# Both norms of an expert stage computed by ScalarE with scales from GpSimd, and early loads on two queues

## The reference

```
h = tok(x)                              # 8 steps of relu(a + shift(state) @ W2.T + b2), both directions
h = h + attention(layernorm(h))         # 8 heads, scores exp(-gamma * |q-k|^2)
n = layernorm(h)
gate = top-2 softmax of n @ gate_w + gate_b
moe  = sum over 16 experts of gate * (relu(n @ w1 + b1) @ w2 + b2)
y = n + moe
h = h + layernorm(y) * gamma + beta
```

## Time and profile before

| | us |
|---|---|
| median of 3 runs | 873.78 |
| lowest and highest | 871.83, 874.65 |
| the profiled execution | 871.59 |
| its span in the trace | 869.0 |

### The profile page before, as it was taken

How to read it: one execution, slowest core, us unless ns; L and a number is a source line. 1 busy time by engine, 2 the same in 40 slices (tenths; PEclk the granted TensorE clock), 3 DMA queues, 4 the chain that set the end, 5 groups by cost and what they waited for, 6 DMA issues and landing times.

```text
span 869.0 us, 16981 instructions
## 1 busy us (share of the span) xinstructions
PE 766.4 (88%) x5712; PEld 438.4 (50%) x5712; DVE 702.2 (81%) x1810; ACT 491.1 (57%) x913; POOL 519.9 (60%) x719
## 2 busy tenths in 40 slices
PE   1699979999999999999999999899889899998894
PEld 1234346666666666666666665344344344444341
DVE  5376768999999999999999998577787877777652
ACT  0365668877887887888788785232333333333221
POOL 7260255445445344454454452469999999999867
PEclk9999979999999999999999999899999999999997
DMA  4300021111221112211112210000000000000000
GB/s 113 136 16 2 1 49 38 36 38 38 49 50 27 39 35 50 50 41 33 38 38 50 49 33 18 1 2 7 8 7 8 7 7 14 7 8 7 8 7 18
DMA packets 22789, 25.71 MB, mean 30 GB/s; under 512 B 12816, under 2 KB 21648, under 8 KB 22576
## 3 DMA queue, kind: packets, MB, share of 16 engines
q1 hardware_dynamic: 22384, 23.85, 11.5%
q10 hardware_dynamic: 320, 0.79, 0.4%
...
## 4 chain that ended last, share of the span: by engine, by line
PE 43%; DVE 33%; POOL 11%; issue 5%; ACT 3%; DMA 2%; SPq 1%; another core or an unknown queue 1%; POOLq 0%; DVEq 0%; ACTq 0%
DVE prob L753 15%; DVE m L769 9%; PE bank L1034 6%; PE bank L962 6%; PE bank L1149 6%; PE bank L1169 6%; PE bank L1082 5%; POOL cxn L425 5%; PE bank L1058 3%; PE bank L1060 2%; DVE qk L763 2%; POOL gated L436 2%; DVE wtok L877 2%; POOL cinv L421 2%; PE bank L1160 2%
## 5 line engine op out<-in xcount | busy, mean ns | idle before, releaser
L753 DVE TENSOR_SCALAR prob<-prob,cap_hi,cap_lo 125x250 f32<-125x250 f32 x512 | 232.7, 502 | 18.6 <-ACT prob L531 15.8
L401 POOL TENSOR_TENSOR sq<-sq 125x256 f32<-125x256 f32 x128 | 96.3, 759 | 170.7 <-ACT sq L545 126.7
L884 DVE SCALAR_TENSOR_TENSOR gated<-bank,nb,wb 128x500 f32<-128x500 f32 x160 | 115.7, 732 | 71.7 <-PE bank L1149 66.4
L1169 PE MATMUL bank<-gated,w_sb 64*64 64x500 f32 x1024 | 172.8, 594 | 0.0
L1149 PE MATMUL bank<-cs,w_sb 64*64 64x500 f32 x1024 | 170.4, 587 | 0.4 <-DVE gated L884 0.4
L531 ACT ACTIVATE prob<-bank 125x500 f32<-125x500 f32 x256 | 148.6, 591 | 38.0 <-PE bank L1060 35.0
L602 ACT ACTIVATE relu<-bank,b_sb 128x500 f32<-128x500 f32 x96 | 65.0, 678 | 175.1 <-PE bank L1149 170.5
L436 POOL TENSOR_TENSOR gated<-relu,wb 128x500 f32<-128x500 f32 x96 | 125.0, 1307 | 48.0 <-ACT relu L602 48.0
L1034 PE MATMUL bank<-prob,u 125*64 125x250 f32 x1024 | 125.8, 382 | 1.5
L1058 PE MATMUL bank<-m,s 128*125 128x500 f32 x256 | 111.0, 434 | 6.1 <-issue 6.1
L1060 PE MATMUL bank<-m,s 112*125 112x500 f32 x256 | 101.0, 395 | 0.0
...
## 6 DMA issues: line engine op xcount, KB each, us to landing
m<-m SPq DMA_DIRECT2D x128, 125.0 KB, 2.3
...
```

Source lines behind the costliest of these rows:

```text
L753: last = dve.tensor_scalar(part, part, cap_hi[0:T, h:h + 1], cap_lo[0:T, h:h + 1], ALU.min, ALU.max)
L884: dve.scalar_tensor_tensor(gated[g % 8][:, :], up_bank(g)[:, 0:C], nb1[:, g:g + 1], wb[q % 2][:, :], ALU.max, ALU.mult).then_inc(c_gated, 1)
L1169: last = pe.matmul(y[cols, 0:C], w2_sb[rows, g, :], gated[g % 8][rows, :], start=g == 1 and rows is HI, stop=v == 7, skip_group_check=True)
```

## The change

Four things are edited.

1. **Norms in stage C.** GpSimd no longer writes `cxn` and `yz`. A new `c_scales(q)`, behind group 1, takes the statistics of pair q and of pair q-4 together (one buffer `cagg` of 8 numbers a partition instead of twice 4) and makes -mean, var + eps, its power and their product. ScalarE then computes `scale * v + bias` with both as per-partition operands: `normed(p+1)`, four instructions on 125x128, and `result(p-3)`, four on 125x64, both in slot 1.
2. **Start, queues.** A_LOADS go from SyncE's queue to ScalarE's, ahead of W_LOADS; a one-element `Relu` stands between them, so that the function table is loaded there. SyncE's queue holds only `x_in`, `xparts`, the replicated copies and B_LOADS, and its wait for GpSimd's fills stands behind the write of `xparts`.
3. **Start, the copies.** The repeat is the second dimension of the source, not the first; rows of weights and constants are reordered to match.
4. **Start, fills.** GpSimd fills all four tails; VectorE's two fills are gone.

```diff
@@ constants
-            rows = slice(half + part * PARTS * D_IN, half + (part + 1) * PARTS * D_IN)
+            rows = slice(half + part, half + XROWS, PARTS)
@@ sync
             sp.dma_start(x_in[:, :, :], xin[:, :, :]).then_inc(a_xin, 16)
-            for dst, src in A_LOADS:
-                sp.dma_start(full(dst), full(src)).then_inc(ld_a, 16)
-
             sp.wait_ge(a_split, SPLIT)
-            sp.wait_ge(s_prepg, PREP_GX)
             sp.dma_start(xparts.rearrange("r p (q l) -> q r p l", q=128), x_part[:, :, :, :]).then_inc(a_scr, 16)
             sp.wait_ge(a_scr, 16)
+            sp.wait_ge(s_prepg, PREP_GX)
...
-                             src.unsqueeze(0).to_broadcast([PARTS, PARTS * D_IN, n * C])).then_inc(s, 16)
+                             src.unsqueeze(1).to_broadcast([PARTS * D_IN, PARTS, n * C])).then_inc(s, 16)
@@ gpsimd
-            done(gp.memset(xa[32:64, :].bitcast(F32), ONES2))
-            done(gp.memset(xw[32:64, :].bitcast(F32), ONES2))
+            for rows in (slice(32, 64), slice(96, 128)):
+                done(gp.memset(xa[rows, :].bitcast(F32), ONES2))
+                done(gp.memset(xw[rows, :].bitcast(F32), ONES2))
...
-            def c_normed(q):
...
+            def c_scales(q):
+
+                if valid(q):
+                    gp.wait_ge(c_ln, 2 * q + 2)
+                if valid(q - 4):
+                    gp.wait_ge(c_fin, 2 * (q - 4) + 2)
+                wait(gp, c_hn, min(q, PAIRS))
+                wait(gp, c_yz, q - 4)
+                gp.tensor_scalar(cneg[:, :, :], cagg[:, :, :, 0], -1.0, None, ALU.mult)
+                gp.tensor_tensor(cvar[:, :, :], cagg[:, :, :, 1], eps2[:, :, :], ALU.add).then_inc(c_inv, 1)
+                gp.wait_ge(c_inv, 3 * q + 1)
+                gp.tensor_tensor(cinv[:, :, :], cvar[:, :, :], mhalf2[:, :, :], ALU.pow).then_inc(c_inv, 1)
+                gp.wait_ge(c_inv, 3 * q + 2)
+                gp.tensor_tensor(cnb[:, :, :], cneg[:, :, :], cinv[:, :, :], ALU.mult).then_inc(c_inv, 1)
...
-                    if n == 0 and valid(p + 1):
-                        c_normed(p + 1)
+                    if n == 0:
+                        c_scales(p + 1)
@@ scalar
+            for dst, src in A_LOADS:
+                act.dma_start(full(dst), full(src)).then_inc(ld_a, 16)
+            act.wait_ge(a_table, 1)
+            act.activation(spare2[:, :], spare[:, :], ACT.Relu)
             act.wait_ge(a_xin, 16)
...
                 if v == 0:
+                    normed(0)
                     tokens_c(0)
...
+            def normed(q):
+
+                act.wait_ge(c_inv, 3 * q + 3)
+                wait(act, c_xt, q)
+                for c in range(CH):
+                    last = act.activation(cxn[:, c, :, :], h_all[:, q * CH + c, :].unsqueeze(1).to_broadcast([T, 2, D]),
+                                          ACT.Identity, bias=cnb[:, 0, c:c + 1], scale=cinv[:, 0, c:c + 1])
+                last.then_inc(c_hn, 1)
+
+            def result(q):
+
+                act.wait_ge(c_inv, 3 * (q + 4) + 3)
+                wait(act, c_gres, 2 * q - 1)
+                for c in range(CH):
+                    last = act.activation(yz[:, 0, c, :], yt[:, c, :], ACT.Identity, bias=cnb[:, 1, c:c + 1],
+                                          scale=cinv[:, 1, c:c + 1])
+                last.then_inc(c_yz, 1)
...
+                if v == 1 and valid(p + 1):
+                    normed(p + 1)
+                if v == 1 and valid(p - 3):
+                    result(p - 3)
@@ vector
-            dve.memset(xa[96:128, :].bitcast(F32), ONES2)
-            dve.memset(xw[96:128, :].bitcast(F32), ONES2)
+            dve.memset(spare[:, :], 0.0).then_inc(a_table, 1)
...
-                wait(dve, c_hn, q)
+                wait(dve, c_inv, 3 * q)
```

More of the change, by code:

```diff
@@ L127, in build @@
         wtok = sb("wtok", [T, CH, E, R])
-        cvar, cinv, cxn = sb("cvar", [T, CH]), sb("cinv", [T, CH]), sb("cxn", [T, CH, 2, D])
+        cagg, cvar = sb("cagg", [T, 2, CH, 2]), sb("cvar", [T, 2, CH])
+        cneg, cinv, cnb, cxn = sb("cneg", [T, 2, CH]), sb("cinv", [T, 2, CH]), sb("cnb", [T, 2, CH]), sb("cxn", [T, CH, 2, D])
+        eps2, mhalf2 = sb("eps2", [T, 2, CH]), sb("mhalf2", [T, 2, CH])
         cs1 = [sb(f"cs1_{j}", [128, C]) for j in range(3)]
@@ L620, in _ @@
             slot_c(0, 7)
-            for p in range(1, PAIRS + 2):
+            for p in range(1, PAIRS + 3):
                 for v in range(8):
```

55 lines of the change are left out of this document (19 added, 36 removed).

## The result

| | us |
|---|---|
| before, median of 4 runs beside it (range) | 872.81 (869.67 to 874.65) |
| after, median of 4 runs (range) | 950.52 (947.66 to 955.08) |
| ratio, 95% interval | 1.0899 (1.0841 to 1.0957) |
| span of the profiled execution, before and after | 869.0 and 950.0 |

The change made the kernel 78 us slower. The forecast was 918 with a range of 887 to 939: the direction held and so did half of the mechanism, the size did not. So the profile after is read for where the other 32 us are.

What follows compares the result with a forecast made beforehand. TensorE was taken to bound stage C, with GpSimd nearly full. Terms -9 + 48 + 1.5 - 0.5 + 4 + 1.5 = +45.5 us gave 917 on the profiled 871.6, 919 on the median 873.8; 918 taken, range 887 to 939.

Steps and rivals of the forecast that it cites:

- piece B: Stage C period after the extra matmuls (L1160): +0.85 us of collision each period, plus 1.2 for the lower clock.
- the collision: After the extra matmuls: freed GpSimd's product of group 9 delays VectorE's step until wtok, +0.85 us a period (0 if missed).
- the clock: Stage C: TensorE's longer idle time brings the lower clock in some eight periods of ten, +1.2 us a period (0 to 2.5).
- start, at step 1 of stage A: Copies spread and issued sooner, weights landing at 18.0, clock gain up to 2: -9 us (bounds -4.5 and -10.5).
- end of stage B: First two token norms on ScalarE, normed(0) and normed(1), delay the end of stage B: together +4 us (1 to 6).
- period 1, period 2: Stage C: period 1 has no y_low yet and gains 0.5 us on cxn; period 2 has only normed, +1.5.
- periods 3 to 14: Stage C periods with both norms: 12 x (1.95 + 0.85 + 1.2) = 12 x 4.0 = +48 us.
- period 15: Stage C before the change, without GpSimd's cxn: read as a trial, 22.23 us against 19.12; no term in the sum.
- from the relu of group 1 of period 16 to the end: Very end of the kernel: ScalarE's last result stands ahead of the last y_low, +1.5 us (-1 to +3).
- Piece A: Stage C, relu of group 1 to the extra matmuls (L1160): y_low queues behind ScalarE's norms, 9.0 to 9.1 against 7.15, +1.95 us.
- The faster rival: Stage C: ScalarE's queue never reaches y_low, TensorE's 1.17 us is gained in 13 periods: 850 us, chance 0.11.
- cheap ScalarE instructions: Stage C rival: eight norm instructions take 1.2 us, piece A falls to +0.76: 904, or 890 without clock loss; chance 0.13.

Runs made afterwards that it cites:

- queue_only: Kernel before with only A_LOADS on ScalarE's queue, the table load and the fills changed, copies in their old form: 872.1 us, ratio 0.9995.
- start_only: Kernel before with only the change's start (queues, table load, fills, copies), expert stage as before: 865.9 us, ratio 0.9937.
- early4: early2 with the token norm of pairs 0 and 1 on GpSimd as before: 841.1 us, ratio 0.9634 to the kernel before.
- early2: Kernel before plus new start, token norm on ScalarE with scales a period early, y_moe before group 5, GpSimd's yz before product 9, results after 12: 844.5 us, 0.9690.
- tail_late: Changed kernel with GpSimd's last two result steps moved from behind the product of group 9 to behind that of group 12: 916.5 us, 1.0508 to before.
- gp_spacer: Changed kernel plus three useless tensor_scalar instructions on GpSimd ahead of its product of group 9: 895.9 us, ratio 1.0290 to the kernel before.
- spacer_tt: Changed kernel plus three useless tensor_tensor instructions on GpSimd ahead of its product of group 9: 978.9 us, ratio 1.1206 to the kernel before.
- fill_short: Changed kernel plus four useless matmuls at each of TensorE's two waits (extra matmuls, wtok transposes): 926.4 us, ratio 1.0618 to the kernel before.

## Why the prediction was wrong

The steps that failed are the two terms of piece B: the collision, put at +0.85 us a period, is +1.84 with the clock up, and the clock, put at +1.2, is 2.5, since a second wait, for `wtok`, was not in the sum. Step by step, on the spans (869.0 and 950.0; +81.0 in all, where the sum had +45.5):

| step | forecast | measured |
|---|---|---|
| start, at step 1 of stage A | -9 | -9.7 |
| end of stage B | +4 | +4.4 |
| period 1, period 2 | -0.5, +1.5 | -1.8, +2.4 |
| periods 3 to 14 | +48 | +76.6 |
| period 15 | none | +4.3 |
| from the relu of group 1 of period 16 to the end | +1.5 | +4.9 |

- *Start*: right in size, in part by luck. The copies landed soon, as said. The DMA share was 0.85 from 16 to 18 us and 1.04 from 18 to 20 where near 0.7 was expected; other transfers ran beside the copies, so no run shows the share of the copies alone. The weights landed 3 us earlier than taken (15.15 for 18.0), and TensorE waited last for the copies, 0.34 us, not for the weights. The "up to 2" of clock was not there: the first `xa` matmuls behind 21.06 take 0.59 to 0.62 us, as before, though the clock column shows 1.00, and 0.37 from 25.10 on. One error made up for the other. Moving the loads gave nothing in the time by itself (`queue_only`), though 3.1 us at step 1.
- *End of stage B*: about right. The 4.4 is the difference between -9.7 and the -5.3 us at which the expert stage's first relu of group 1 stands, and 1.3 of it `start_only` loses too, without the norms. `early4` against `early2` puts the first two norms alone at 2.3 us by that relu (537.55 against 539.83) and at 3 to 5 by times and ratios.
- *Piece A*: right, 9.2 for 9.05 to 9.1. Power 1.66 (1.5 taken, in the bounds), `cxn` to the relu of group 4 2.88 (2.75), `y_low` at 7.86 (7.8). The faster rival needed 5.4 there and is out; so is the one of cheap ScalarE instructions, whose 1.2 us for eight no row had shown. TensorE's wait for `cxn` stayed at 0.71, where under 0.5 was expected.
- *Piece B, collision, +0.85: the first step that failed.* It was read from L866 of period 15 alone, and fits that period by luck. There L866, L870 and L873 are held, 0.98 + 0.27 + 0.53 = 1.78 us, where the usual period of before has 0.95 (L873 0.53, `wtok` 0.42); the difference is the 0.82 by which `wtok`'s transposes are late. `wtok` itself was free in period 15, since it began just ahead of a product:

```profile
831.53 0.68 DVE L877 TENSOR_TENSOR wtok<-lg 125x512 f32<-125x512 f32 x1
831.61 1.72 POOL L436 TENSOR_TENSOR gated<-relu,wb 128x500 f32<-128x500 f32 x1 [0.73 <-ACT relu L602]
```

  So it is in the six periods of after where the slower clock put the product of group 12 off (4.93 us, third row of the pieces). In the other six `wtok` is held too: 0.98 + 0.27 + 0.53 + 1.01 = 2.79 us, 1.84 more than before, as the third row shows (5.95 against 4.11). The collision and the clock were added as if they did not touch. That period 15 also had a wait of 1.48 us for `wtok` where 0.83 is usual was passed over. `tail_late`, `gp_spacer` and `spacer_tt` show the holds.
- *Piece B, clock, +1.2: the second.* For the wait that was foreseen it is about right: a fall behind `y_moe`'s wait came in 8 of 12 periods, and in six of them costs 24.52 - 23.01 = 1.5 us, since the late product then spares `wtok` (4.93 in place of 5.95). Not foreseen was a second fall, behind `wtok`'s wait of 2.67: in 6 of 12 periods, at 26.04 - 23.01 = 3.0. Together 2.5 a period, as `fill_short` shows. Without the extra holds there is no such wait and no such fall: `gp_spacer`, whose filler keeps them away, won 55 us.
- Together: (1.84 - 0.85) + (2.5 - 1.2) = 2.3 us, and 2.4 with piece A's 0.1, in 12 periods the 28.6 of the 35.5 missing. *Period 15* (+4.3) and the *end* (+3.4 over the forecast) make up the rest: the sum had set period 15 to nothing, as if the trial were itself unchanged, while ScalarE's `yz` and the wait of 2.67 with its lower clock come there too.
- *Range*: the clock had an upper bound, 2.5, and piece A one, but the collision had only a lower one, 0. With 1.84 and 2.5 the sum comes to +73, about 945.

What stays open: why a wait of 2.42 us is followed by the lower clock in some periods and not in others (5 of 12 in `gp_spacer`, 8 of 12 in after, 9 of 12 in `tail_late`, all in `spacer_tt`); why GpSimd's power does not hold VectorE; and what delays the step by 0.35 us in period 14.
